# One normaliser pipeline in a fused attention and FFN kernel: strip passes of means and variances side by side with the scores, weighing ahead of the tiles, rows of means sent ahead of q's weights

## The reference, cut to what matters

```python
h = einsum('bct,bcd->bdt', x, cond_w[subjects])      # a 64 x 64 matrix per sequence
q, k, v = h @ Wq, h @ Wk, h @ Wv                     # 512 -> 16 heads of 128
beta = sigmoid(h @ Wb + bb); gate = silu(h @ Wg)
q = layernorm(silu(causal_dwconv(q, 4 taps)))        # per head, with weight and bias
k = layernorm(silu(causal_dwconv(k, 4 taps)))
S_t = (1 - beta_t) S_{t-1} + beta_t v_t k_t^T ; o_t = S_t q_t    # scan over 64 tokens
x = x + (o * gate) @ Wo
y = x @ W2^T + adapter of rank 16                    # adapter chosen per sequence
x = x + bias + int8_quantized(rmsnorm(y)) @ ternary(ffn_w)^T * scales
```

## Time and profile before

| | |
|---|---|
| median of 3 runs | 2570.62 us (2568.57 to 2571.15) |
| the profiled execution | 2573.15 us, of which 2571.4 us are the span from its first to its last instruction |
| TensorE (PE) busy | 2450.2 us, 95% of the span, 14292 matmuls |
| VectorE (DVE) | 1633.6 us, 64% |
| ScalarE (ACT) | 1072.2 us, 42% |
| GpSimd (POOL) | 783.9 us, 30% |
| mean granted clock of TensorE | 0.979 of full speed |
| DMA | 551.38 MB, 214 GB/s; the queue that SyncE feeds fills 62.2% of 16 engines' span |

### The profile page before, as it was taken

One profiled execution on the slowest core, in us unless ns is written; L12 is line 12 of the kernel. 1 busy time (PEld: TensorE's weight loads), 2 busy tenths in 40 slices (PEclk: granted clock), 3 DMA queues, 4 the chain that ended last, 5 costly groups with the idle time before them and its releaser, 6 DMA issues. The chain is left out here.

```text
span 2571.4 us, 38384 instructions
## 1 busy us (share of the span) xinstructions
PE 2450.2 (95%) x14292; PEld 1849.9 (72%) x14292; DVE 1633.6 (64%) x2653; ACT 1072.2 (42%) x1615; POOL 783.9 (30%) x636
## 2 busy tenths in 40 slices
PE   7789899999999999999999999999999999999976
PEld 5567677777777777777777777777777777777754
DVE  4666456676667756576566766667666775657653
ACT  4554444444435334443434434444443533444321
POOL 3465433322323222232233232232132322223230
PEclk9899999999999999999999999999999999999987
DMA  7786766567665776666676676656757577666750
GB/s 233 255 309 220 258 224 231 194 204 258 201 222 185 238 232 199 207 202 226 212 231 196 201 249 212 222 187 219 253 192 228 186 231 233 205 203 203 228 173 17
DMA packets 326962, 551.38 MB, mean 214 GB/s; under 512 B 98354, under 2 KB 122970, under 8 KB 326778
## 3 DMA queue, kind: packets, MB, share of 16 engines
q1 hardware_dynamic: 315778, 529.75, 62.2%
q10 hardware_dynamic: 11000, 19.18, 2.3%
HBM read 495.08 MB, written 53.74 MB: 213 GB/s over the span
## 5 line engine op out<-in xcount | busy, mean ns | idle before, releaser
L526 POOL TENSOR_TENSOR og_lo<-gt,og_hi 128x512 fp32r<-128x512 f32 x128 | 181.6, 1418 | 1128.3 <-ACT og_hi L1040 1128.3
L1110 PE MATMUL pj_a<-ht_hi,wq 128*128 128x512 f32 x1024 | 361.3, 414 | 30.8 <-ACT gt L1033 21.3
L1110 PE MATMUL pj_a<-ht_hi,wg 128*128 128x512 f32 x1024 | 355.5, 408 | 17.2 <-DMA wg<-parts_g 12.9
L812 DVE SCALAR_TENSOR_TENSOR y_q<-pj_a,conv,y_q 128x504 f32<-128x504 f32 (+2 forms) x384 | 281.1, 732 | 137.9 <-ACT y_q L1016 128.7
L1110 PE MATMUL pj_b<-ht_hi,wk 128*128 128x512 f32 x1024 | 346.7, 399 | 8.4 <-DMA wk<-parts_k 8.3
L1110 PE MATMUL ring<-wo,og_hi 128*128 128x512 f32 x1024 | 324.3, 398 | 5.2 <-issue 5.2
L1110 PE MATMUL ring<-wv,ht_hi 128*128 128x512 f32 x1024 | 320.5, 394 | 4.5 <-POOL wv L516 4.5
L812 DVE SCALAR_TENSOR_TENSOR y_k<-pj_b,conv,y_k 128x504 f32<-128x504 f32 (+2 forms) x384 | 281.4, 733 | 56.0 <-ACT y_k L1016 46.8
L522 POOL TENSOR_TENSOR y_k<-y_k,sq_k 128x512 f32<-128x512 f32 x128 | 170.8, 1335 | 462.2 <-DMA sq_k<-m_rows 462.1
L1110 PEld LDWEIGHTS pj_b<-ht_hi,wk 128*128 128x128 f32 x1024 | 192.4, 188 | 107.1 <-issue 52.0
L1110 PEld LDWEIGHTS pj_a<-ht_hi,wq 128*128 128x128 f32 x1024 | 197.6, 193 | 80.2 <-issue 24.9
(11 more groups left out here) (202 smaller groups left out, 4645.6 us busy)
## 6 DMA issues: line engine op xcount, KB each, us to landing
wq<-parts_q SPq DMA_DIRECT2D x112, 512.0 KB, 4.2
wk<-parts_k SPq DMA_DIRECT2D x112, 512.0 KB, 6.2
wg<-parts_g SPq DMA_DIRECT2D x112, 512.0 KB, 5.9
wv<-parts_v SPq DMA_DIRECT2D x112, 512.0 KB, 6.5
wo<-parts_o SPq DMA_DIRECT2D x112, 512.0 KB, 6.7
sq_q<-m_rows SPq DMA_DIRECT2D x110, 256.0 KB, 3.8
sq_k<-m_rows SPq DMA_DIRECT2D x110, 256.0 KB, 4.5
sq_q<-r_rows SPq DMA_DIRECT2D x110, 256.0 KB, 3.5
```

Of the source, the lines that this page charges most:

```text
L526: G.tensor_tensor(og_lo[:, u % OG_RING, :], gt[:, u % GT_RING, :], og_hi[:, u % OG_RING, :].bitcast(F32), ALU.subtract).then_inc(S["oglo"], 1)
L812: V.scalar_tensor_tensor(out=yy[:, :, k:], in0=pp[:, :, :L - k], scalar=conv[:, i, h, 3 - k:4 - k], in1=yy[:, :, k:], op0=ALU.mult, op1=AL ...
L1110: last = T.matmul(psum, a, b, start=start and n == 0 and m == 0, stop=stop and n == len(pairs) - 1 and m == 2)
```

## The change

From slot 20 on (`ROWS_SP`): on TensorE the means come after k instead of before it, and the scores come right behind the strip passes, ahead of the first tiles. On VectorE `weigh` comes ahead of the first tiles' use. On ScalarE `keep_means` comes behind k's first tap. On SyncE the rows of means are sent ahead of q's load. The slots before 20 keep their order.

```diff
@@ SyncE
+                if U % 2 == 0 and ROWS_SP <= U <= UNITS:
+                    send_means(U // 2 - 1)
                 if H <= U + 1 < UNITS:
                     load_head("q", U + 1)
-                if U % 2 == 0 and ROWS_SP <= U <= UNITS:
-                    send_means(U // 2 - 1)
                 if H <= U + 1 < UNITS:
                     load_head("k", U + 1)
@@ VectorE
+                if ROWS_SP <= U < UNITS + 4:
+                    weigh(U - 4)
                 take(U, 0)
-                if 0 <= U - 4 < UNITS:
+                if 4 <= U < ROWS_SP:
                     weigh(U - 4)
@@ ScalarE
-                if U % 2 == 0 and 2 <= U <= UNITS:
+                if U % 2 == 0 and 2 <= U < ROWS_SP:
                     keep_means(U // 2 - 1)
-                    if U < ROWS_SP:
-                        send_means(U // 2 - 1)
+                    send_means(U // 2 - 1)
...
                 if U < UNITS:
                     first_tap("k", U)
+                if U % 2 == 0 and ROWS_SP <= U <= UNITS:
+                    keep_means(U // 2 - 1)
@@ TensorE
-                if U % 2 == 0 and 2 <= U <= UNITS:
+                if U % 2 == 0 and 2 <= U < ROWS_SP:
                     means(U // 2 - 1)
                 if U < UNITS:
                     project("k", U)
                 if U % 2 and 3 <= U <= UNITS + 1:
                     variance((U - 3) // 2)
+                elif U % 2 == 0 and ROWS_SP <= U <= UNITS:
+                    means(U // 2 - 1)
+                if ROWS_SP <= U < UNITS + 4:
+                    score(U - 4)
                 make(U, 0)
-                if 0 <= U - 4 < UNITS:
+                if 4 <= U < ROWS_SP:
                     score(U - 4)
```

## The result

The changed kernel takes 2648.55 us (median; 2643.95 to 2662.7), the kernel before beside it 2570.89 us: 77.7 us slower, ratio 1.0306 with a 95% interval of 1.028 to 1.0333. The forecast was slower, 2612 us with a range to 2634: the sign was right, about half of the size was missing, and the result lies outside the range.

What follows compares the result with a forecast made beforehand. TensorE, busy almost without a gap, was taken to bound the kernel. The terms -23 - 19.9 + 3.2 + 22.8 + 11.0 + 44.6 + 2.9 gave +41.6 us, a median of 2612 us; 80% range 2573 to 2634.

Steps and rivals of the forecast that it cites:

- Joining the narrow blocks: TensorE, slots 20 to 127: scores directly behind strips save one opening and one closing, 0.23 us a slot; -23 us taken.
- Affine results: Scores wait for GpSimd's result (line 533): slot 8 0.46 us late, slot 10 3.25; seven rounds, +3.2 and +22.8 us.
- Gate-out: Slot 9: VectorE frees m0, the bank the scores write, 1.57 us late; seven rounds, +11.0 us.
- The queue of SyncE: q's load waits behind the rows' write and broadcasts; q's weights come late in 33 short even slots, 1.35 us each, +44.6 us.
- Waits that go: TensorE's old waits in slots 20 to 127, for wk 8.3, wg 9.5 and a transposed tile 2.1 us, vanish: -19.9 us.
- Slot 128: No projections there; scores wait for the affine result, TensorE standing 5.09 us instead of 2.21: +2.9 us.
- Clock: Rival, chance 0.17: slot 10's 3.25 us pause halves TensorE's clock, 17 us more, 2629 us; with slot 128's pause 2631.
- the upper bound of q's wait: Short even slots: q's weights late by 2.2 us each, 73 us in all, if the rows' write lands later.

Runs made afterwards that it cites:

- the run with late scores: Changed kernel with scores and weighing in their old place in slots 8, 9 and 10 of each group and slot 128: 2623.25 us.
- filling the pause: Changed kernel with slot 10's strip passes of means done four times over, same result: 2636.3 us, the change beside it 2661.03 us.
- The filled pauses: Changed kernel with slot 10's strip passes repeated (2636.3 us), unused matmuls before waits for q's weights in 33 odd slots (2642.55 us), or both (2625.88 us).
- the kernel with both parts undone: Changed kernel with q's load ahead of the rows again and scores and weighing in their old place in slots 8, 9, 10 and 128: 2557.47 us.

## Why the prediction was right or wrong

- "Joining the narrow blocks", -23 us: right. Short slots without a wait are 16.70 us, the junction costs 1.00 us, and the 85 slots at the full clock are 0.23 us shorter on average, waits subtracted, the price of the forecast. Moving the scores of the odd slots alone gains 7.2 us where the price says 10.3.
- "Affine results" and "Gate-out", 3.2, 22.8 and 11.0 us: right, 3.3, 22.6 and 11.5 measured.
- "The queue of SyncE", 44.6 us for 33 slots: the mechanism is right and the total is close, 46.4 in 31. The steps 7.43, 9.14 and 17.87 us were measured in slot 52 as 7.42, 9.42 and 17.4. The closeness of the total is in part luck: the slots in question are 34 and not 33, three of them show no wait, the broadcasts start later than written and q lands sooner behind them, slot 52 itself waits 0.68 us and not 1.17, the single waits run from 0.25 to 3.06 us, and in the second trace of the same kernel they are 51.5 us up to slot 127. Undoing this part alone takes 56 us off, the clock behind it included.
- "Waits that go", -19.9 us: right. But the run with late scores shows a link that the sum did not have: slot 10's pause covers q of slot 11.
- "Slot 128", +2.9 us: from the start of slot 127 to the end it is 4.7 us longer (2650.9 - 2524.5 against 2571.4 - 2449.7); its scores wait 5.19 us where 5.09 was forecast, and the tile behind runs at the lower clock.
- The step that failed is the clock. The sum gave it nothing, and the rival "Clock" gave it 17 us, for slot 10 alone. Measured are about 33.5 us in slots 20 to 126, with 19 stretches at 1.2 GHz where before had none. For slot 10 the rival was near: 13.7 us in the trace of the change, and 12.4 by filling the pause. Two things were wrong in the working. First, the sum left the clock out on the evidence that waits of up to 2.7 us had left it up; but of those 21 waits one was above 2 us (2.73), so the rows said little about a pause of 3.25. Behind the attention's narrow matmuls, twelve of the 31 waits for wq, from 1.25 us on, did bring it down. Second, neither the sum nor the rival put the lower clock behind the waits for wq, which bring twelve of the 19 stretches, though these waits were in the same sum. The filled pauses show that this is the cause: the same gate for the scores, and 25 and 18.5 us less beside the change on one chip, each with all or most of the stretches at its own waits gone. The Trainium skill, page "TensorE: Matmul & The Clock Gate", section "Why this matters for your kernels", warned of idle gaps between bursts; slot 10's pauses of 3.24 us agree, each with a stretch at the lower clock behind it.
- The range was too narrow by its own terms: it names the clock and the upper bound of q's wait for its top of 2634, but the upper bound of 73 us alone gives 2612 + 28 = 2640, and with the 17 us of the clock 2657, which would have let the result in.

The 33.5 us are what is left of the measured time, so that the sum with them, 2612 + 33.5 = 2645.5 us, comes near the median is no proof. What places them is the count by slots, 29.7 us more in the 22 slots with the lower clock, and the filled pauses.

Left open: which wait brings the clock down. Waits of the same length do and do not, and from run to run it is others. The change's first four runs spread over 19 us and its two medians, on two chips, are 12 us apart, so differences of that size between runs on different chips say little; before's runs spread over 10 to 12 us, on one chip over 22. Why the median of the kernel with both parts undone gained 12.8 us, when its traced run is 18 us under before's median and the slots explain that, stays open.

## What to carry to other kernels

Where one engine is full, price a new wait on it twice: its length, and what the work behind it loses at the lower clock; here that was about 34 us on top of 84 us of new waits. More than half of it came with waits for q's weights, each of them shorter than the pause of slot 10 that alone had looked dangerous. A step moved forward spends the cover in front of it, so ask for each operand when it is there in the slots that are behind for other reasons; here three of sixteen slots ate what the other thirteen gained. And ask before a small transfer with a landing to wait for is put ahead of a large load with a near due time, in a list that is issued in order: here that cost 41 us by itself.

## What the runs showed of the hardware

TensorE gets faster when its pause is filled with useless matmuls: the tile behind a 3.24 us pause took 4.57 us, behind the same pause filled up to the last 0.68 us 3.09. A wait of 2.81 us in front of a projection cost 1.6 us more than its length (4.44 instead of 2.85), one of 2.70 us cost nothing more. A pass of four strip matmuls into four column groups cost 1.00 us when the scores follow, and less when repeated: four such passes took 4.32 us with 0.68 idle, 0.91 each. In the changed kernel twelve of the 31 waits for wq (0.25 to 3.06 us, behind narrow matmuls) had a stretch at 1.2 GHz with them, the shortest of the twelve 1.25 us long; the pauses of 3.24 us in slot 10 had one seven times in seven, and with q's load first six times in seven.
